# Four attention blocks on one core: seven PSUM banks as one pool, an exponential for each half of a pair, and a new table of steps

## The reference, cut to what matters

```python
x = _L0_conv_ref(x, ...)   # group norm (16 groups), 8 heads of 16 channels, + x
x = _L1_conv_ref(x, ...)   # group norm (32 groups), 8 heads of 16 channels, + the normed x
x = _L2_conv_ref(x, ...)   # layer norm, one head of 128 channels, + x
x = _L3_conv_ref(x, ...)   # group norm (32 groups), one head of 128 channels, + x

# a block with heads, for each image and head
scores = jnp.einsum('bcq,bck->bqk', q, k) * hd ** (-0.5)     # 1024 x 1024
scores = jax.nn.softmax(scores, axis=-1)
o = jnp.einsum('bqk,bck->bqc', scores, v)
out = jnp.einsum('bhwc,cd->bhwd', o, w_out) + b_out
return out + skip
```

## Time and profile before

| | before |
|---|---|
| median of 3 runs (lowest to highest) | 2158.66 us (2158.46 to 2170.19) |
| the profiled execution: its own time, its span | 2159.86 us, 2158.1 us |
| granted PE clock, mean | 0.986 of full speed |
| busy: PE, DVE, ACT, POOL | 97%, 78%, 67%, 19% |
| DMA | 97.34 MB, mean 45 GB/s |

### The profile page before, as it was taken

How to read it: one execution, slowest core, us unless ns; L and a number is a source line. 1 busy time by engine, 2 the same in 40 slices (tenths; PEclk the granted TensorE clock), 3 DMA queues, 4 the chain that set the end, 5 groups by cost and what they waited for, 6 DMA issues and landing times.

```text
span 2158.1 us, 39609 instructions
## 1 busy us (share of the span) xinstructions
PE 2096.4 (97%) x15750; PEld 1168.3 (54%) x15750; DVE 1687.8 (78%) x3104; ACT 1447.0 (67%) x1698; POOL 408.0 (19%) x541
## 2 busy tenths in 40 slices
PE   4999999999999999999999999999999989999999
PEld 2444444444744467444764448644584336746888
DVE  6899999999799867887679886898778957763433
ACT  1477777777577755887458874688647865586554
POOL 3102111220122311122120221213111040130221
PEclk7799999999999999999999999999999999999999
DMA  5322241331222314041230503204040050000000
GB/s 144 70 31 66 48 96 46 65 72 29 55 55 56 45 31 79 12 85 16 55 65 2 99 2 70 50 2 99 1 103 7 2 99 1 11 2 1 11 1 20
DMA packets 48583, 97.34 MB, mean 45 GB/s; under 512 B 7824, under 2 KB 10640, under 8 KB 48272
## 3 DMA queue, kind: packets, MB, share of 16 engines
q1 hardware_dynamic: 48400, 94.81, 21.0%
HBM read 55.98 MB, written 37.75 MB: 43 GB/s over the span
## 4 chain that ended last, share of the span: by engine, by line
PE 84%; DVE 8%; DMA 2%; issue 2%; ACT 2%; POOL 1%; SPq 1%; POOLq 0%; DVEq 0%; ACTq 0%
PE outs L1430 21%; PE work L1376 17%; PE pairs L1404 12%; PE outs L1470 11%; PE pairs L1448 8%; DVE part_max L1168 6%; PE pairs L1292 6%; PE pairs L1298 3%; PE pairs L1301 2%; PE work L1298 2%; DMA q_stack<-shift_parts 2%; PE work L1301 2%; ACT probs L1057 1%; DVE neg_max L1200 1%; SPq L853 1%
## 5 line engine op out<-in xcount | busy, mean ns | idle before, releaser
L1168 DVE TENSOR_REDUCE part_max<-work 128x1 f32<-128x512 f32 x2048 | 1282.7, 681 | 176.1 <-PE work L1376 169.6
L1057 ACT ACTIVATE probs<-pairs 128x1024 f32<-128x1024 f32 x1024 | 1002.1, 1023 | 261.2 <-PE pairs L1404 244.4
L1376 PE MATMUL work<-k_stack,q_stack 62*128 62x512 f32 x2048 | 609.7, 453 | 5.9 <-DVE part_max L1168 3.8
L1430 PE MATMUL outs<-probs,v_heads 128*32 128x512 f32 (+1 forms) x5216 | 565.8, 512 | 0.8 <-DVE o_turn L1180 0.2
L1404 PE MATMUL pairs<-q_stack,k_stack 64*128 64x512 f32 x2048 | 509.0, 446 | 15.4 <-DMA q_stack<-shift_parts 14.0
L1376 PEld LDWEIGHTS work<-k_stack,q_stack 62*128 62x128 f32 x2048 | 286.9, 187 | 316.3 <-DVE part_max L1168 233.0
L1404 PEld LDWEIGHTS pairs<-q_stack,k_stack 64*128 64x128 f32 x2048 | 224.9, 185 | 220.1 <-ACT probs L1057 128.8
L1200 DVE TENSOR_REDUCE neg_max<-pairs 128x1 f32<-128x1024 f32 x128 | 156.7, 1224 | 207.4 <-PE pairs L1448 206.7
L1064 ACT ACTIVATE probs<-pairs,neg_max 128x1024 f32<-128x1024 f32 x128 | 142.8, 1116 | 241.0 <-DVE neg_max L1200 241.0
L1470 PEld LDWEIGHTS outs<-v_full,probs 128*128 128x128 f32 x2048 | 250.8, 191 | 37.3 <-issue 28.8
L1470 PE MATMUL outs<-v_full,probs 128*128 128x128 f32 x2048 | 269.7, 279 | 0.2
(11 more groups left out here) (128 smaller groups left out, 1157.2 us busy)
## 6 DMA issues: line engine op xcount, KB each, us to landing
k_scratch<-parts SPq DMA_DIRECT2D x64, 256.0 KB
q_scratch<-parts SPq DMA_DIRECT2D x64, 256.0 KB
k_stack<-k_scratch SPq DMA_DIRECT2D x64, 256.0 KB, 6.9
q_stack<-q_scratch SPq DMA_DIRECT2D x64, 256.0 KB, 9.6
k_stack<-k_scratch SPq DMA_DIRECT2D x64, 128.0 KB, 8.1
q_stack<-q_scratch SPq DMA_DIRECT2D x64, 128.0 KB, 10.2
q_stack<-shift_parts SPq DMA_DIRECT2D x256, 4.0 KB
tmp<-x SPq DMA_DIRECT2D x7, 512.0 KB, 3.8
```

What stands on the lines that cost most here:

```text
L1057: nc.scalar.activation(probs[:, plan.prob[u], 2 * n:2 * n + 2, :], pairs[:, plan.half["pair", t], :, :], ACT.Exp, scale=HEAD_SCALE).then_i ...
L1168: nc.vector.tensor_reduce(part_max[:, r % 2, column:column + 1], bank_of(("tile", r, n)), AX_X, ALU.max, negate=True).then_inc(tile_max, 1)
L1376: nc.tensor.matmul(bank_of(("tile", r, n)), qs[rows, i, a, heads, P * t:P * (t + 1)], ks[rows, i, keys, heads, :], start=True, stop=True). ...
L1430: last = nc.tensor.matmul(outs[2 * HD * n:2 * HD * (n + 1), columns], v_heads[:, i, key, at:at + 2 * HD], probs[:, plan.prob[u], n, column ...
```

## The change

1. The three banks of `work` and the four of `pairs` become one tensor `banks` of seven. `Banks.take` gives an item the bank, or the two neighbouring banks, whose last handing out lies longest back, and remembers who held them; PE waits for each of these holders (`wait_for_banks`).
2. The two matmuls of a P take a bank each, which need not be neighbours, wait each for their own, and report each for itself (`pair_full` counts two for a P). ACT takes the exponential of each half in an instruction of its own, 128x512 in place of 128x1024, so 2048 in place of 1024. In full stages a P still takes two neighbouring banks.
3. S, R, G and y have letters and queues of their own, and the string `STEPS` is another one. It has 10 items fewer, since there are 642 V and U in place of 652.

The work on DVE and POOL, the DMAs and the data are the same.

```diff
@@ -26,7 +26,9 @@
 SLOTS = KT * ROUNDS
 TILES = GROUP * KT
 PROB_RING = 3
-WORK_BANKS = 3
+BANKS = 7
+SINGLES = {"head": {"work": (0, 1, 2, 3, 4, 5, 6), "exp": (0, 1, 2, 3, 4, 5, 6)}, "full": {"work": (0, 1, 2, 3, 4, 5, 6)}}
+DOUBLES = {"head": ((0, 1), (1, 2), (2, 3), (3, 4), (4, 5), (5, 6)), "full": ((0, 1), (1, 2), (2, 3), (3, 4), (4, 5), (5, 6))}
...
@@ -68,6 +70,42 @@
 
 def kind_of(name):
     return name if name in ("gn1", "gn2") else name.rstrip("01")
+
+
+class Banks:
+
+    def __init__(self):
+        self.holders, self.last, self.count = [None] * BANKS, [-1] * BANKS, 0
+
+    def take(self, choices, holder):
+
+        chosen = min(choices, key=lambda banks: max(self.last[b] for b in banks))
+        before = []
+        for b in chosen:
+            if self.holders[b] is not None and self.holders[b] not in before:
+                before.append(self.holders[b])
+            self.holders[b], self.last[b] = holder, self.count
+        self.count += 1
+        return chosen, before
+
+    def take_for(self, plan, item, part):
+
+        if item[0] in ("scores", "turn"):
+            return [self.take(DOUBLES["full"], item)]
+        if item[0] == "pair" and part == "full":
+            (first, second), before = self.take(DOUBLES["full"], (*item, 1))
+            self.holders[first] = (*item, 0)
+            return [((first,), before), ((second,), before)]
+        if item[0] == "pair":
+            return [self.take([(b,) for b in SINGLES[part]["exp"]], (*item, k)) for k in range(2)]
+        if plan.in_pairs(item) and item[1] not in HALVES:
+            return [self.take(DOUBLES[part], item)]
+        user = "exp" if plan.in_pairs(item) and part == "head" else "work"
+        return [self.take([(b,) for b in SINGLES[part][user]], item)]
+
+
+def part_of(item, part):
+    return "full" if item[0] in ("scores", "turn", "pv") else "head" if item[0] == "values" else part
 
 
 class Plan:
@@ -107,67 +145,67 @@
     FIRST_STEPS = "C" * 29 + "T" * 36 + "C" * 1 + "T" * 4
     STEPS = (
         "TPTPTTTPTCUTPTU TTPTCCUTPTU TTPTCCUTPTU TTPTCCUTPTU TTPTCCUTPTU CTPTCCUTPTU TTPTPCUTTU TPTPCCUTTU CTPTTPTV "
-        "TPTTPV TPTTPTV TPTPUTTU TPTPUTTU CTPTPTV TPTTUPTTU TTPPTTV CPPTTTUU PTTUTPTU TTPPTUTTU PPTTTV TTPPTV "
...
+        "TPTTPV TPTTPTV TPTPUTTU TPTPUTTU CTPPTTV TTPPTUTTTTU TPPUU CTPTTPV TPTTTTPUPTU TPTTTUU PTTPUTPTU TPTTCV "
...
     def arranged(self, order):
 
-        queues = {n: deque(c for c in order if n == self.class_of(c)) for n in "TPC"}
+        queues = {n: deque(c for c in order if n == self.class_of(c)) for n in "TPCSRGY"}
...
     def class_of(self, item):
-        return {"tile": "T", "pair": "P", "values": "V"}.get(item[0], "C")
+        return {"tile": "T", "pair": "P", "values": "V", "scores": "S", "turn": "R", "pv": "G", "y": "Y"}.get(item[0], "C")
...
-            if self.in_work(item):
-                bank = n % WORK_BANKS
-                n += 1
-                self.bank[item], self.before[item] = bank, held.get(bank)
-                held[bank] = item
-            elif self.in_pairs(item):
-                self.half[item] = ring % 2
-                ring += 1
-                self.pairs_before[item] = pairs_held.get(self.half[item])
-                pairs_held[self.half[item]] = item
+            part = part_of(item, part)
+            if self.in_work(item) or self.in_pairs(item):
+                taken = banks.take_for(self, item, part)
+                self.banks[item] = sum((chosen for chosen, _ in taken), ())
...
-        pairs = psum("pairs", [P, 2, 2, HALF])
+        banks = psum("banks", [P, BANKS, HALF])
         outs = psum("outs", [P, HALF])
-        work = psum("work", [P, WORK_BANKS, HALF])
...
                     if n == 0:
                         probs_free(("exp", u))
-                    act.wait_ge(pair_full, t + 1)
-                    nc.scalar.activation(probs[:, plan.prob[u], 2 * n:2 * n + 2, :],
-                                         pairs[:, plan.half["pair", t], :, :], ACT.Exp,
-                                         scale=HEAD_SCALE).then_inc(exp_done, 1)
+                    for k, half in enumerate(halves_of(t)):
+                        act.wait_ge(pair_full, 2 * t + k + 1)
+                        nc.scalar.activation(probs[:, plan.prob[u], 2 * n + half, :],
+                                             banks[:, plan.banks["pair", t][k], :], ACT.Exp,
+                                             scale=HEAD_SCALE).then_inc(exp_done, 1)
 
                 def full_exp(n):
                     act.wait_ge(f_max, n + 1)
...
             @block.tensor
             def _(pe):
-                def wait_for_bank(item):
-                    before = plan.before[item]
-                    if before is None:
-                        return
-                    if before[0] == "tile":
-                        pe.wait_ge(tile_max, plan.tile_nth[before] + 1)
-                    elif before[0] == "shift":
-                        pe.wait_ge(*taken(*before))
-                    else:
-                        pe.wait_ge(*taken(*before[1:]))
+                def wait_for_banks(item, k=0):
+                    for before in plan.before[item][k]:
+                        if before[0] == "tile":
+                            pe.wait_ge(tile_max, plan.tile_nth[before] + 1)
+                        elif before[0] == "pair":
+                            pe.wait_ge(exp_done, 2 * before[1] + before[2] + 1)
+                        elif before[0] == "scores":
+                            pe.wait_ge(f_exp, before[1] + 1)
+                        elif before[0] == "turn":
+                            pe.wait_ge(f_copied, before[1] + 1)
+                        elif before[0] == "shift":
+                            pe.wait_ge(*taken(*before))
...
-                    wait_for_pairs(("pair", t))
-
-                    start = plan.rows_first["pair", t]
-                    for half in (start, 1 - start):
+                    for k, half in enumerate(halves_of(t)):
                         rows = slice(ROWS * half, ROWS * (half + 1))
-                        last = nc.tensor.matmul(pairs[:, plan.half["pair", t], half, :],
-                                                ks[rows, i, key // QT, first + n, P * (key % QT):P * (key % QT + 1)],
-                                                qs[rows, i, a, first + n, :], start=True, stop=True)
-                    last.then_inc(pair_full, 1)
+                        wait_for_banks(("pair", t), k)
+                        nc.tensor.matmul(banks[:, plan.banks["pair", t][k], :],
+                                         ks[rows, i, key // QT, first + n, P * (key % QT):P * (key % QT + 1)],
...
                     columns = slice(HALF // 2 * start, HALF // 2 * (start + count))
-                    pe.wait_ge(exp_done, 2 * (u + 1))
```

More of the change, by code:

```diff
@@ L470, in count @@
     def count(self):
-        self.bank, self.before, held, n = {}, {}, {}, 0
+        self.banks, self.before, banks, part = {}, {}, Banks(), "head"
         self.use, self.takes, self.chunks = {}, {}, []
@@ L719, in bank_of, with halves_of @@
         def bank_of(item):
-            if item in plan.bank:
-                return work[:, plan.bank[item], :]
-            both = pairs[:, plan.half[item], :, :]
-            return both[:, 0, :] if item[0] == "chunk" and item[1][-1] in "01" else both.rearrange("p a k -> p (a k)")
+            first, last = plan.banks[item][0], plan.banks[item][-1]
+            if first == last:
+                return banks[:, first, :]
+            return banks[:, first:last + 1, :].rearrange("p a k -> p (a k)")
+        def halves_of(t):
+            first = plan.rows_first["pair", t]
+            return first, 1 - first
         def tiles_of(half):
@@ L1357, in shift @@
                 def shift(r):
[L1358 removed]
+                    wait_for_banks(("shift", r))
                     pe.wait_ge(max_ready, r + 1)
```

147 lines of the change are left out of this document (67 added, 80 removed).

## The result

The changed kernel takes 2099.93 us in the median (2093.61 to 2111.09, four runs), the kernel before 2158.56 beside it (2158.07 to 2170.19): a ratio of 0.9727, with a 95% interval of 0.9694 to 0.9759. Forecast were 2129 and a range of 2107 to 2160.

The account below looks back on a forecast made before the run. PE was taken as the bound, with DVE setting the pace in the first stages. 42.0 us saved by order, less 6 (first stages), 2 (last slots) and 4 (pool), gave 30: 2129 us, range 2107 to 2160.

Parts of the forecast that it names:

- PE's order: On PE: the new order of matmuls, with 1465 stretches in place of 1603, saves 42.0 us.
- prices: PE's time per stretch of matmuls, by mix and without waits: 1993 us of the 2158.1 us span before the change.
- What the first stages keep: Five head stages up to 575 us: DVE sets the pace, so 6 of 12.9 us saved are given back.
- The exponentials: On ACT: halves take 0.60 us, start 0.50 apart, add 74 us, hidden by PE except 2 us.
- the last slots: Slots after the last T, where ACT itself is the bound: half exponentials lose 2 us.
- The pool: Seven shared banks: waits about as tight but of more kinds, 4 us lost; bounds minus 20 to plus 40.
- PE is at its prices there, so this gives nothing: Full stages: S and R drawing on seven banks in place of four gains nothing.
- "spread" waits: Some 100 of PE's 165 us of waits, those not ahead of the first P or in one DMA wait.
- What doesn't go: The wait for the shift's DMA, 11.56 us to landing, and the start at DVE's pace both stay.
- Rival 1: The pool couples DVE and ACT, costing 34 us in place of 4: 2159 us, no change; chance 0.17.
- Rival 2: ACT becomes the bound because half exponentials don't overlap, 0.28 us more per P: 2189 us; chance 0.10.
- Rival 3: Halves freed separately and longer T runs make 24 more of the 100 us vanish: 2105 us; chance 0.13.

Follow-up runs that it names:

- the last experiment: Changed kernel with the last two reads of stacked keys and queries moved behind the shift of round 59: 2092.31 us, ratio 0.9691 to the kernel before.

## Why the prediction was wrong, by its own steps

- **PE's order, 42.0 us: right.** That the prices of before and after differ by 42.0 tests nothing, since it is the same sum; but the stretches keep their times, and the experiment with 64 more changes of shape moved the time by 23.4 for 21.6.
- **"What the first stages keep", 6 us given back: failed.** Stages 0 to 4 took 13.2 us less, all that their prices save (12.9), and their waits went from 45.7 to 45.4. The step took a busy DVE for one that sets the pace. DVE went from 96.5 to 98.5% in stage 2 without holding PE up more, and its own waits for T between the first P and stage 5 fell from 26.1 to 20.0 us. By stage the sum hides a little: the waits grow by 3.0 us in stages 0 to 2 and shrink by 3.3 in 3 and 4. Of the 3.0, 1.6 are stage 1 with its late shift and slow clock; in the last experiment, with the same order up to there, a shorter wait (1.37 us) and the clock at full speed, stage 1 took 90.4 us for 93.0. So this part is the shift and not DVE.
- **The exponentials: right in what matters, mis-sized.** 0.61 us each as forecast (0.60), but 0.48 apart for 0.50: 0.04 us for each P in place of 0.07, and 43 us of ACT for 74. It stays hidden. Of the 2 us for the last slots 0.4 show, less than stage 15 differs between two traces (0.9). On the kernel before, the halves alone cost 0.29%.
- **"The pool", plus 4: failed, in two ways.** As a part by itself it was too small: under the old order pool and halves add 18 us of waits up to stage 14, and the halves alone 3.7. In the changed kernel it was too large, since the new order takes them back: its waits up to stage 14 are 137.0 us for 141.5. Adding the two terms as if they were independent was the error; the terms of order and pool cannot be priced apart (always with halves: +162 us for the order alone, +15 for the pool alone, -59 for both).
- **"PE is at its prices there, so this gives nothing": failed, and the largest single error.** It was said of all full stages. In the last stretch the price was 181.5 us and the time 198.0, so 16.5 us of the "spread" waits stood in one place that the windows would have shown. The pool took 8.0 of them, the order 3.5; the halves have no part in it, since this stretch is 186.5 us with one exponential for a pair too.
- **"What doesn't go": right.** The late shift stayed (8.66 us for 9.51 of PE), and the start, from PE's first load to the first stretch with P, took 60.4 for 61.8. That it had to stay is another matter: two reads moved from ahead of it give 8 to 10 us, as the last experiment shows.
- **The rivals.** Rival 1 (coupling) doesn't show in the changed kernel, though its parts can bring it: some 14 us of waits with pool and halves under the old order, and far more with one exponential for a pair (130 us) or with six banks (240). Rival 2 (ACT) doesn't happen: the halves overlap. Rival 3 (waits go, 2105) came nearest. It had 24 us of waits vanish, and 15.6 did; it put them on the freed halves and longer T runs everywhere, while 11.1 of them lay in the last part, where halves have no share.

Put together: 30 forecast, 12 us of losses that did not come, 15.6 us of waits that went, and 1 us over, 58.6. Each of the small terms erred to the same side. The range was also narrower than its own parts: with nothing lost in the first stages and the last slots, and the pool at its lower bound of minus 20, the prediction's sum comes to 2097, and its third rival stood at 2105; the range began at 2107.

It stays open why up to stage 14 pool and new order together wait no more than separate banks and old order did: the experiments show that they fit (seven banks, not six; halves, not pairs), not which of the items would be the first to wait. Two rivals were not run: pairs in neighbouring banks that are read and given back by halves, and another rule for which bank is handed out next.

## What to carry to other kernels

Price an engine's work by stretches, subtract the prices from each stage's time, and look where the rest lies before a pool, a buffer or an order is called worthless there; one stretch of 198 us held a tenth of all waits. A static order and the buffers that it runs on are one design: here, always with halves, the order without the pool costs 7.5%, the pool without the order 0.7%, and both together gain 2.7%, so a part that loses by itself says nothing on the whole. Where several engines share a ring of buffers, try it in the smallest unit that an instruction can do with: here the larger unit cost 83 us under one order and 130 under the other. And follow a wait for a small DMA to what was issued ahead of it: two reads moved behind the shift gave 8 to 10 us.

## What the runs showed of the hardware that was not expected

- Shorter exponentials overlap more: of 512 columns (0.609 us) the next starts 0.48 us later, 0.13 us before the end; of 1024 (1.023) it was 0.92, so 0.10. The Trainium skill, page "ScalarE: Activation LUTs", section "What ACT_TABLE_LOAD costs", has 93 ns for that; the trace agrees for 1024 columns and not for 512.
- 0.37 us for each pair of changes between rows and columns of the array, 23.4 us for 64 (0.34 by the price list). The Trainium skill, page "TensorEngine Tiling (Array Packing)", section "Key Properties", says that a change of mode drains the engine; these runs agree with a cost at each change and give the price.
- A DVE that is busy 98.5% of a stage need not hold up PE: with seven banks in common PE's waits in stage 2 were 6.6 us of 87, for 6.3 at 96.5%.
- Behind waits of PE for DMAs the granted clock fell to 0.50: for 10.2 us in and behind one of 8.66 us, for 3.4 us behind one of 2.57. The first cost 2.1 us on top of the wait.
- Four small DMAs behind 16 reads were waited for until 12.7 us after the first was issued (1719.91 to 1732.66); with eight of the reads moved behind them, PE found them there after 4.9 us.
